# A vision tower on one core: attention that forms its scores a second time by keys, two fused mixer fronts and a scan with wider jobs

## The chip, the cores and the metric

The kernel runs on one core of one Trainium2 chip, in one launch. The metric is the device time in microseconds (us) of an execution. The engines are PE (TensorE: matrix products and transposes into PSUM), DVE (VectorE), ACT (ScalarE), POOL (GpSimd) and SP (SyncE, which issues transfers). PE's clock is granted at one of two levels, 1.2 or 2.4 GHz; the profile gives it as a share of full speed, 0.50 or 1.00 (a number between is a mean over a stretch).

## What is computed

32 images become 32 x 50 = 1600 tokens of 192 features, and four layers follow, each a mixer and a feed-forward part (ffn), each added to the stream h. Everything is fp32. The diff touches four mixers:

```python
# layer 0 mixer: a bilinear state-space scan, 16 states per feature
bc = x @ W_bc;  delta = softplus(x @ W_dt @ W_dtp + b_dt)
delta = delta * rsqrt(mean(delta * delta) + 1e-6) * rms_scale
dE = soft_clamp(delta, 0.0001, 10.0)             # centre + half_range * tanh(...)
half = 0.5 * dE * A;  denom = 1.0 - half          # A = -exp(A_log)
A_bar = (1.0 + half) / denom;  B_bar = sqrt(dE) * B_sel / denom
Bx = B_bar * 0.5 * (x + x_prev);  h_t = A_bar * h_(t-1) + Bx;  y = sum(C * h) + D * x
# layer 1 (inside its ffn) and layer 2 (its mixer): attention of 12 heads of 16
attn = softmax(q @ k.T * scale)                   # within one image of 50 tokens
out = (attn @ v) @ proj_w + proj_b                # in layer 2 q and k are of unit length first
# layer 3 mixer: 384 inner features
x_s, z = split(rms(x) @ w_in);  xc = silu(conv4(x_s) + conv_b)
B, C, log_dt = split(xc @ w_xproj);  dt = softplus(log_dt @ w_dt + b_dt)
h_t = exp(dt * A) * h_(t-1) + dt * B * xc;  y = (sum(C * h) + D * xc) * silu(z) @ w_out
```

The other parts (patch embedding, layer 1's one-head mixer, the expert layers) are as in the reference, and the diff leaves them.

## The kernel before, in words

`tower` calls the stages one after another. A stage is one or more blocks (`t.block()`): in a block each engine has its own program, they meet only in semaphores (`wait_ge`, `then_inc`), and a block ends for all engines together. So nothing of one block overlaps the next, and the order on an engine is the order in which its program is written; `Fori` is a loop on the engine itself. Tokens are worked in 16 tiles of 100 (two images) or in 4 chunks of 400. `h` and `x` hold tokens on partitions, `xT` holds features on partitions, 96 and 96.

- **Layer 0's front** (`layer0_mixer`, from L695). Block one (L708): per chunk PE forms `bc` (L718), the rank-48 product (L721) and, when ACT has copied that (L741), the rate (L727). Block two (`softplus`, L372, 8 spans of 200 tokens): ln(1+e^z) from Abs, Exp, Ln and one more Exp on ACT (L385 to L398) and five steps on DVE (L405 to L421). Block three (L760): per chunk a square (L766), the mean over features on PE (L781), Sqrt (L768), reciprocal on DVE (L797), two scalings (L800); then over all tokens at once Tanh (L770), clamp (L804), Sqrt (L773) and the input u (L807).
- **The scan** (`scan`, L428). First B and C are split into three bf16 parts (L453 to L459). Then a job is one state of one group of features over a chunk. In layer 0 there are 2 groups of 96 partitions, so 32 jobs a chunk; DVE does three instructions a job: `weigh` (L613), the recurrence (L622) and `read` (L628), with ACT making the decay (L533, L540, L548), POOL one product (L586), and PE spreading B and C over partitions (L493) and summing the states with an identity (L489). In layer 3 there are 3 groups of 128 and 48 jobs.
- **Attention** (`heads_attention`, L1092; layer 1 with unit=False, layer 2 with unit=True). One tile an iteration, two in flight. PE projects q, k, v (L1153, L1154), transposes q and k to 6 blocks (L1160), forms 12 score blocks, four at a time on 16 rows each (L1169); DVE scales, masks and copies the scores to SBUF (L1313) and takes the maximum (L1318), POOL subtracts it (L1130), ACT takes the exponent (L1252), DVE sums (L1331); PE transposes the 12 probability blocks (L1198), ACT copies them (L1268), PE forms probabilities x values with 16 moving columns (L1209); the result is divided by the sums (L1339), transposed (L1216), projected (L1220, L1221) and added (L1347). In layer 2 ACT squares (L1232), DVE sums (L1288) and bounds (L1292) the lengths, and ACT takes their inverse root.
- **Layer 3's front** (`layer3_mixer`, L2005). Per chunk PE forms the 6 input products (L2030), ACT copies three (L2052) and takes silu of three (L2056), DVE does the convolution (L2075, L2077), then silu (L2059), `xproj` (L2035), a copy (L2062), the rate (L2041, L2085), and only then the next chunk. `softplus` follows as a block of its own, then one DVE product over all tokens (L2097).

## Time and profile before

| what | us |
|---|---|
| median of three runs (3040.43 to 3058.68) | 3053.26 |
| the profiled execution | 3052.19 |
| its span in the trace | 3050.1 |
| PE busy, share of the span | 2350.0, 77% |
| DVE busy | 1462.9, 48% |
| ACT busy | 980.4, 32% |
| POOL busy | 798.6, 26% |
| granted clock of PE, mean | 0.768 |

A row of a timeline has the start, the time from the first start to the last end of the merged instructions, engine, line, operation, output and inputs, their number, and in brackets the idle time before them and who ended it. PEld is the loading of the stationary operand, which runs beside PE. An fp32 product is two records in the trace. Transposes in fp32 are one record.

### The profile page before, as it was taken

The page shows a single profiled execution, that of the slowest core. Times are in us where ns is not written, and L with a number is a line of the kernel's source. Part 1 is how long each engine was busy: PE and PEld are TensorE (multiplying, and loading weights), DVE is VectorE, ACT ScalarE, POOL GpSimd, SP SyncE. Part 2 cuts the span into 40 slices and gives each one's busy share as a digit, 9 for nine tenths or more (in the row PEclk, how much of TensorE's full clock was granted, in tenths as well). Part 3 has the DMA queues.
Part 4 walks back from the last instruction along what each step waited for, and adds up shares of the span by engine and source line. Part 5 has one row for each costly group of instructions (what it writes and reads, how often), then busy time and mean ns, then how long its engine had stood idle before and what let it go on. Part 6 is the DMA issues. An engine that isn't in the chain of part 4 may idle for free. (4 is left out here: it accounts for less than half of the span.)

```text
span 3050.1 us, 44650 instructions
## 1 busy us (share of the span) xinstructions
PE 2350.0 (77%) x12100; PEld 1653.3 (54%) x12100; DVE 1462.9 (48%) x3230; ACT 980.4 (32%) x2061; POOL 798.6 (26%) x781
## 2 busy tenths in 40 slices
PE   9617997975897597699779954477756993699998
PEld 9302333653675486477536722122245982699987
DVE  4269996234455311555521254899953224422222
ACT  1147784122233233233221223455522221222211
POOL 0004551001122054111100000477602441244443
PEclk9655555876676599555589976799967995799999
DMA  7000000000000386000012100000006761577775
GB/s 205 3 0 1 0 0 0 0 0 0 1 0 0 92 212 152 12 0 0 0 31 62 31 0 0 1 0 0 0 9 193 223 178 42 179 223 223 224 214 128
DMA packets 77597, 201.30 MB, mean 66 GB/s; under 512 B 17685, under 2 KB 47256, under 8 KB 69176
## 3 DMA queue, kind: packets, MB, share of 16 engines
q1 hardware_dynamic: 52472, 169.30, 17.3%
q0 software_dynamic: 25056, 31.22, 6.1%
q8 instruction: 26, 0.43, 0.1%
q14 instruction: 43, 0.35, 0.0%
HBM read 178.81 MB, written 22.91 MB: 66 GB/s over the span
## 5 line engine op out<-in xcount | busy, mean ns | idle before, releaser
L489 PE MATMUL bank<-g,consts 128*128 128x400 f32 (+1 forms) x640 | 388.6, 703 | 64.3 <-DVE g L628 58.6
L1502 POOL DMA_INDIRECT sums<-yblock,put x129 | 206.0, 1597 | 421.0 <-DVE yblock L1765 249.3
L622 DVE TENSOR_TENSOR_SCAN s<-bank,w 128x400 f32<-128x400 f32 (+1 forms) x320 | 313.2, 979 | 3.9 <-POOL w L597 3.8
L1550 PE MATMUL bank<-xTblock,wt 128*128 128x256 f32 (+1 forms) x1464 | 268.4, 341 | 1.7 <-ACT xTblock L1621 1.2
L1755 DVE TENSOR_TENSOR hid<-sa,bank 128x512 f32<-128x512 f32 (+1 forms) x183 | 105.9, 578 | 340.7 <-ACT sa L1642 337.8
L1575 PE MATMUL bank<-wt,hid 128*128 128x192 f32 x1548 | 265.6, 326 | 0.0
L489 PEld LDWEIGHTS bank<-g,consts 128*128 128x128 f32 (+1 forms) x640 | 117.5, 220 | 269.8 <-DVE g L628 260.1
L597 POOL TENSOR_TENSOR w<-u,spreadB 128x400 f32<-128x400 f32 x192 | 192.8, 1036 | 242.1 <-ACT spreadB L568 242.1
L1550 PEld LDWEIGHTS bank<-xTblock,wt 128*128 128x128 f32 x1464 | 237.3, 194 | 23.7 <-issue 1.6
L1575 PEld LDWEIGHTS bank<-wt,hid 128*128 128x128 f32 x1548 | 249.8, 190 | 0.2
L1642 ACT ACTIVATE sa<-bank 128x512 f32<-128x512 f32 (+1 forms) x183 | 93.3, 510 | 482.2 <-PE bank L1561 477.3
L363 PE MATMUL bank<-consts,xs 100*96 100x100 f32 x320 | 71.2, 383 | 168.8 <-DVE xs L316 130.1
L586 POOL TENSOR_TENSOR w<-u,r 96x400 f32<-96x400 f32 x128 | 132.2, 1034 | 258.0 <-ACT r L540 245.6
L1497 POOL DMA_INDIRECT xblock<-table,take x135 | 134.9, 999 | 223.8 <-DVE put L1731 175.2
L493 PE MATMUL bank<-thirds,select 96*96 (+1 forms) x256 | 90.3, 441 | 111.9 <-ACTq L524 66.4
L628 DVE TENSOR_TENSOR g<-s,bank 128x400 f32<-128x400 f32 (+1 forms) x320 | 175.5, 549 | 0.1
L1130 POOL TENSOR_TENSOR scores<-scores,red 100x1200 f32<-100x1200 f32 x34 | 74.6, 2194 | 344.5 <-DVE red L1318 344.5
L552 ACT ACTIVATE bank<-rate,coef 128x392 f32 x192 | 113.2, 591 | 117.8 <-DVE s L622 117.8
L363 PEld LDWEIGHTS bank<-consts,xs 100*96 100x96 f32 x320 | 38.8, 175 | 201.7 <-DVE xs L316 154.8
L1765 DVE TENSOR_SCALAR yblock<-bank,gate 128x192 f32<-128x192 f32 x129 | 49.4, 414 | 205.1 <-PE bank L1575 205.1
L1561 PE MATMUL bank<-xTblock,wt 64*128 64x256 f32 (+1 forms) x1464 | 143.2, 342 | 0.0
L493 PEld LDWEIGHTS bank<-thirds,select 96*96 96x96 bf16 (+1 forms) x256 | 33.0, 129 | 201.0 <-issue 192.0
(364 smaller groups left out, 4062.9 us busy)
## 6 DMA issues: line engine op xcount, KB each, us to landing
wt<-L3f_packed SPq DMA_DIRECT2D x41, 1152.0 KB, 5.8
wt<-L3f_packed SPq DMA_DIRECT2D x41, 576.0 KB, 6.0
wt<-L3m_packed SPq DMA_DIRECT2D x20, 1152.0 KB, 5.6
wt<-L_packed SPq DMA_DIRECT2D x20, 579.0 KB, 4.4
wt<-L3m_packed SPq DMA_DIRECT2D x20, 577.0 KB, 5.9
wt<-L_packed SPq DMA_DIRECT2D x20, 576.0 KB
pixels<-pixels SPq DMA_DIRECT2D x16, 375.0 KB, 4.3
wu<-L_up SPq DMA_DIRECT2D x8, 576.0 KB, 4.6
```

Source lines behind the costliest of these rows:

```text
L489: nc.tensor.matmul(acc[g][0:parts, 0:CHUNK], ident[0:parts, 0:parts], g_[:, j % SLOTS, :], start=(n == 0), stop=(n == STATES - 1)).then_in ...
L493: return nc.tensor.matmul(bank[0:parts, 0:CHUNK], select[:, row:row + 1].to_broadcast([6 * STATES, parts]), thirds[:, at], start=True, sto ...
L552: nc.scalar.activation(rest, rate[:, g, at].rearrange("p (b t) -> p b t", t=SEQ)[:, :, 1:SEQ], ACT.Exp, scale=coef[:, g, n:n + 1]).then_in ...
L586: nc.gpsimd.tensor_tensor(w1[:, j % SLOTS, :], u[:, j % groups, at], r[:, j % SLOTS, :], ALU.mult).then_inc(w1_done, 1)
L597: nc.gpsimd.tensor_tensor(w2[:, j % SLOTS, :], u[:, g, at], spreadB[:, n % 2, :], ALU.mult).then_inc(bu_done, 1)
L622: nc.vector.tensor_tensor_scan(s[:, j % SLOTS, :], decays[j % DECAYS], w2[:, j % SLOTS, :], 0.0, ALU.mult, ALU.add).then_inc(s_done, 1)
L628: nc.vector.tensor_tensor(g_[:, j % SLOTS, :], s[:, j % SLOTS, :], bankC[(j // groups) % 2][0:parts, 0:CHUNK], ALU.mult).then_inc(g_done, 1)
L1497: nc.gpsimd.indirect_dma_start(x[:, b % 2, q - column_of_block[b], :], None, table, bass.IndirectOffsetOnAxis(take[:, q:q + 1], 0)).then_i ...
L1502: nc.gpsimd.indirect_dma_start(t.sums, bass.IndirectOffsetOnAxis(put[:, q:q + 1], 0), y[:, b % 2, q - column_of_block[b], :], None, comput ...
L1550: nc.tensor.matmul(bank[:, n * j:n * (j + 1)], wt[:, v, cols(base, 2 * p + j)], xT[:, v, 0, 0:n], start=(j == 0), stop=False, skip_group_c ...
L1561: last = nc.tensor.matmul(bank[:, n * j:n * (j + 1)], wt[half, v, cols(REST_AT, 2 * p + j)], xT[half, v, 1, 0:n], start=False, stop=True, ...
L1575: last = nc.tensor.matmul(bankY[s], hid[:, m, 128 * s:128 * (s + 1)], wt[:, v, DOWN_AT + DIM * m:DOWN_AT + DIM * (m + 1)], start=(m == 0 a ...
```

## The change

What it does, part by part:

1. **Layer 0's normalise is wide.** `xT` becomes 128 partitions x 2: features 0 to 127, and features 128 to 191 written twice (64 and 64 partitions). Each tile gets one more DVE instruction (64 columns). The row of ones that was set once in `embed` is set by POOL in layer 0's `add_back`.
2. **Layer 0's front is one block** of 7 unrolled steps over 4 chunks: chunk n is projected, n-2 is in softplus, n-3 is scaled. The root of the mean is Exp(-0.5 Ln(mean + 1e-6)) on ACT, reading PSUM; the reciprocal on DVE is gone. Every operation is now on 128 partitions and 800 columns a chunk. x + x_prev is on POOL. Tanh, clamp, Sqrt and u go by chunks.
3. **Layer 0's scan** (`bilinear_scan`) has 24 jobs a chunk: 16 of the first 128 features, and 8 that hold two states of the last 64. B and C are spread once a job, the second kind with a stationary operand `select_pair` made once (96 x 2048), and its states are summed with a folded identity.
4. **Attention** (both layers) forms the scores twice. The first time (L1363, 18 rows: two more carry the mask) only DVE's maximum reads them, from PSUM, and writes it as a column of the wide q. That is transposed again (3 blocks), and the second score product (L1371, 19 rows) has keys as output partitions, with mask and shift in the product, so ACT takes the exponent from PSUM in one instruction of 1200 columns and its result is already transposed. The sums and the outputs are 24 products with a stationary operand of 32 columns (ones, or the padded values) and 100 moving columns at column positions 0, 32, 64, 96 (L1380). The reciprocal is Exp(-Ln) on ACT, the division leaves `aT` ready for three projection products and one for the bias (L1418, L1419). POOL's subtraction, the 12 transposes of probabilities and their copies, the DVE masking, sum and reciprocal, and the transposes of the result are gone. The projection weights arrive by a transfer in this block.
5. **Layer 3's front is one block** of 6 unrolled steps: chunk n projected, n-1 mixed, n-2 in softplus; ACT changes its table twice a step; u is formed by POOL chunk by chunk. Layer 3's scan is unchanged.

```diff
-        self.xT = sb("xT", [HALF + 1, 2, TOKENS + 2 * TILE])
+        self.xT = sb("xT", [128, 2, TOKENS + 2 * TILE])
...
+                        if wide:
+                            nc.vector.tensor_scalar(xs[:, u:u + 1, DIM:LINE], src[:, at, 128:DIM], mv[:, at, 0:1], sd[:, 2, at],
+                                                    ALU.subtract, ALU.mult)
...
+def job_states(j):
+
+    p, r = divmod(j, 3)
+    return (1, (2 * p, 2 * p + 1)) if r == 2 else (0, (2 * p + r,))
...
+                            lhs = select_pair[:, (base + states[0]) // 2].rearrange("p a b -> p (a b)")
+                        return nc.tensor.matmul(bank[:, 0:CHUNK], lhs, thirds[:, at], start=True, stop=True)
...
-                    with act.Fori(0, CHUNKS) as c:
-                        at = bass.ds(CHUNK * c, CHUNK)
-                        act.sem_inc(t.passed, 1)
-                        nc.scalar.activation(sq[:, :, at], rate[:, :, at], ACT.Square).then_inc(squared, 1)
-                        act.wait_ge(eps_done, c + 1)
-                        nc.scalar.activation(rms[:, 1, :], rms[:, 0, :], ACT.Sqrt).then_inc(root, 1)
...
+                        c = n - 2
+                        if live(c):
+                            act.wait_ge(soft, c + 1)
+                            nc.scalar.activation(sq[:, c], rate[:, :, at(c)], ACT.Square).then_inc(squared, 1)
+                        c = n - 3
+                        if live(c):
+                            act.wait_ge(meant, c + 1)
+                            nc.scalar.activation(rms[:, 0, c % 2, :], bank_mean[c % 2][:, 0:CHUNK], ACT.Ln, bias=w["eps6"]).then_inc(logged, 1)
...
+                def score_turned():
+                    for g in range(GROUPS):
+                        for j in range(4):
+                            rows = slice(32 * j, 32 * j + DEEP)
+                            last = nc.tensor.matmul(bankS[j][0:TILE, TILE * g:TILE * (g + 1)], qkT[rows, 1, g, :], shiftedT[rows, g, :],
+                                                    start=True, stop=True)
+                    last.then_inc(scoredT, 1)
+
+                def weigh(v):
+                    for bank in (bankR, bankO):
+                        for g in range(GROUPS):
+                            for j in range(4):
+                                rows = slice(32 * j, 32 * (j + 1))
+                                last = nc.tensor.matmul(bank[rows, TILE * g:TILE * (g + 1)],
+                                                        ones[:, 0:2 * HEAD] if bank is bankR else v_[:, v, 4 * g + j, :], pT[:, j, g, :],
+                                                        start=True, stop=True, tile_position=(0, 32 * j))
+                    last.then_inc(weighed, 1)
...
+                        act.wait_ge(scoredT, n + 1)
+                        nc.scalar.activation(pT[:].rearrange("p j g n -> p j (g n)"), wholeS, ACT.Exp).then_inc(exp_done, 1)
+                        act.wait_ge(weighed, n + 1)
+                        nc.scalar.activation(logs[:].rearrange("p g n -> p (g n)"), bankR[:, 0:GROUPS * TILE], ACT.Ln).then_inc(sums_logged, 1)
+                        act.wait_ge(sums_logged, n + 1)
+                        nc.scalar.activation(inv[:], logs[:], ACT.Exp, scale=-1.0).then_inc(inv_done, 1)
+                        square(n + 2)
+                        take_shifted(n + 1)
+                        root(n + 2)
...
+                        take_qkT(n + 1)
+                        highest(n + 1, 1 - u)
+                        dve.wait_ge(inv_done, n + 1)
+                        nc.vector.tensor_tensor(aT[:].rearrange("p g n -> p (g n)"), bankO[:, 0:GROUPS * TILE],
+                                                inv[:].rearrange("p g n -> p (g n)"), ALU.mult).then_inc(a_done, 1)
+                        lengths(n + 2)
+                        take_qk(n + 2, u)
+                        take_v(n + 2, u)
+                        dve.wait_ge(out_done, n + 1)
...
-                        pe.wait_ge(rate_done, G * c + G)
...
+                @block.gpsimd
+                def _(pool):
+                    for c in range(CHUNKS):
+                        pool.wait_ge(soft, c + 1)
+                        nc.gpsimd.tensor_tensor(u[:, :, at(c)], rate[:, :, at(c)], xc[:, :, at(c)], ALU.mult)
```

**Where instructions stand, first place: PE, one tile of the attention loop of layer 1.** The numbers are those of the listing; the first listing is the kernel before, with L1169 the scores, L1153 and L1154 the projection, L1198 the transposes of probabilities, L1160 those of q and k, L1209 the values, L1216 to L1221 the output.

```order
305 L1169 MATMUL bank<-qkT 100x100 x12
...
307 L1153 MATMUL bank<-consts,xtile 100x384
308 L1154 MATMUL bank<-consts,xtile 100x384
309 L1153 MATMUL bank<-consts,xtile 100x192
310 L1154 MATMUL bank<-consts,xtile 100x192
...
313 L1198 MATMUL bank<-consts,scores 100x100 x12
314 L1160 MATMUL bank<-consts,wide 128x100 x6
...
316 L1209 MATMUL bank<-v,probsT 100x16 x4
...
321 L1216 MATMUL bank<-consts,a 96x100 x2
322 L1220 MATMUL bank<-consts,aT 100x192
323 L1221 MATMUL bank<-consts,aT 100x192
```

In the changed kernel L1371 is the second score product, L1363 the first, L1380 the 24 narrow products, L1349 the transposes of q, k and shifted q:

```order
318 L1371 MATMUL banks<-shiftedT,qkT 100x100 x12
...
320 L1349 MATMUL banks<-consts,wide 128x100 x6
321 L1363 MATMUL banks<-qkT 100x100 x12
322 L1380 MATMUL banks<-probsT,ones 32x100 x12
323 L1380 MATMUL banks<-probsT,v 32x100 x12
...
325 L1342 MATMUL banks<-consts,xtile 100x384
326 L1343 MATMUL banks<-consts,xtile 100x384
327 L1342 MATMUL banks<-consts,xtile 100x192
328 L1343 MATMUL banks<-consts,xtile 100x192
329 L1349 MATMUL banks<-consts,wide 128x100 x3
330 L1418 MATMUL banks<-wproj,aT 100x192 x3
331 L1419 MATMUL banks<-wproj,ones 100x192
```

The 12 transposes of probabilities are gone, a second set of 12 score products has come, and the transposes of q and k stand ahead of the first scores of the next tile.

**Second place: PE, layer 3's front, the first two chunks.** Before, with L2030 the input products, L2035 `xproj` and L2041 the rate; these rows are a loop's body, run once a chunk:

```order
646 L2030 MATMUL bank<-xT,consts 128x400
...
648 L2030 MATMUL bank<-xT,consts 128x400 x11
...
651 L2035 MATMUL bank<-xc,consts 33x400
...
653 L2035 MATMUL bank<-xc,consts 33x400
...
655 L2035 MATMUL bank<-xc,consts 33x400
...
657 L2041 MATMUL bank<-bc_203,consts 128x400 x3
```

Now, unrolled, with L2222 and L2231 the input products of x and z, L2240 `xproj` and L2248 the rate:

```order
628 L2222 MATMUL banks<-xT,consts 128x400 x6
629 L2231 MATMUL banks<-xT,consts 128x400 x6
630 L2222 MATMUL banks<-xT,consts 128x400 x6
631 L2231 MATMUL banks<-xT,consts 128x400 x6
632 L2240 MATMUL banks<-xc,consts 33x400 x3
633 L2248 MATMUL banks<-bc_211,consts 128x400 x3
```

The 12 input products of the second chunk now stand ahead of the first chunk's `xproj` and rate.

## Rows read from the trace of the kernel before

**Rows 1.** Stretches of stages: us; busy PE, PEld, DVE, ACT, POOL; clock; DMA.

```profile
111.50:228.70 117.20, 46.31 (x64) 12.36 (x64) 51.35 (x71) 37.56 (x56) 0.00 (x0) 0.50 0.00 0
228.70:236.50 7.80, 0.00 (x0) 0.00 (x0) 7.22 (x7) 0.00 (x0) 0.00 (x0) 0.50 0.00 0
242.80:491.50 248.70, 235.25 (x381) 77.02 (x381) 240.94 (x391) 195.91 (x377) 130.45 (x127) 0.50 0.00 0
757.80:965.20 207.40, 186.18 (x1332) 141.88 (x1332) 100.40 (x186) 60.19 (x118) 44.03 (x36) 0.70 0.00 0
1243.50:1480.60 237.10, 215.90 (x1332) 167.92 (x1332) 128.64 (x240) 74.63 (x172) 44.02 (x36) 0.57 0.00 0
1792.80:1930.00 137.20, 61.31 (x144) 29.26 (x144) 67.29 (x102) 43.30 (x69) 0.00 (x0) 0.70 0.00 0
1950.00:1962.00 12.00, 9.55 (x25) 3.27 (x24) 12.00 (x19) 6.39 (x12) 9.02 (x10) 1.00 0.00 1
```

**Rows 2.** Timeline of layer 0's front.

```profile
112.12 2.87 PE L718 MATMUL bank<-xT,consts 96*32 x4 [1.49 <-PEq L712]
...
119.04 2.95 PE L727 MATMUL bank<-low,consts 48*96 x4 [1.22 <-ACT low L741]
...
196.66 2.65 DVE L797 RECIPROCAL rms<-rms 96x400 f32<-96x400 f32 x1 [0.60 <-ACT rms L768]
...
225.06 3.49 DVE L807 SCALAR_TENSOR_TENSOR u<-u,sq 96x3200 f32<-96x3200 f32 x1 [2.94 <-ACT sq L773]
```

**Rows 3.** Groups of instructions of the scans: xcount, then busy us and mean ns.

```profile
L622 DVE TENSOR_TENSOR_SCAN s<-bank,w 128x400 f32<-128x400 f32 (+1 forms) x320 | 313.2, 979 | 3.9 <-POOL w L597 3.8
...
L628 DVE TENSOR_TENSOR g<-s,bank 128x400 f32<-128x400 f32 (+1 forms) x320 | 175.5, 549 | 0.1
```

**Rows 4.** Timeline of layer 0's scan, PE.

```profile
350.94 0.87 PE L493 MATMUL bank<-thirds,select 96*96 x2
...
351.61 3.22 PE L489 MATMUL bank<-g,consts 96*96 96x400 f32 x4
```

**Rows 5.** Timeline of layer 1's attention, PE.

```profile
859.29 0.79 PE L1169 MATMUL bank<-qkT 16*100 16x100 f32 x24
...
860.00 1.60 PE L1153 MATMUL bank<-consts,xtile 97*100 97x384 f32 x2
...
863.96 2.21 PE L1198 MATMUL bank<-consts,scores 100*100 100x100 f32 x12
...
866.92 2.21 PE L1209 MATMUL bank<-v,probsT 100*100 100x16 f32 x24
...
871.98 1.09 PEld L1169 LDWEIGHTS bank<-qkT 16*100 16x100 f32 x24 [0.48 <-issue]
...
871.98 1.34 PE L1169 MATMUL bank<-qkT 16*100 16x100 f32 x24
```

**Rows 6.** Groups of instructions of attention.

```profile
L1313 DVE SCALAR_TENSOR_TENSOR scores<-bank,consts 100x300 f32<-100x300 f32 x136 | 52.8, 450 | 6.3 <-PE bank L1169 6.3
...
L1318 DVE TENSOR_REDUCE red<-scores 100x12 f32<-100x1200 f32 x34 | 47.7, 1403 | 1.2
...
L1252 ACT ACTIVATE scores<-scores 100x1200 f32<-100x1200 f32 x34 | 40.7, 1197 | 0.0
...
L1245 ACT ACTIVATE qkT<-bank 128x300 f32<-128x300 f32 x72 | 26.3, 418 | 65.3 <-PE bank L1160 65.1
...
L1292 DVE TENSOR_SCALAR norm<-norm 100x24 f32<-100x24 f32 x18 | 14.9, 829 | 0.6
```

**Rows 7.** Timeline of layer 3's front, all engines.

```profile
1793.51 1.28 ACT L2047 ACT_TABLE_LOAD   x1 [0.27 <-PEq L99]
...
1794.03 10.62 PE L2030 MATMUL bank<-xT,consts 96*128 x24 [2.15 <-PEq L2024]
...
1806.58 2.17 PE L2035 MATMUL bank<-xc,consts 128*33 x6 [1.93 <-ACT xc L2059]
...
1924.60 5.16 DVE L2097 TENSOR_TENSOR u<-rate,xc 128x4800 f32<-128x4800 f32 x1 [0.32 <-PEq L99]
```

More of the change, by code:

```diff
@@ L271, in _, with normalise @@
                     last.then_inc(multiplied, 1)
-def normalise(t, src, eps, *, keep=None, centred=True, gain=None, bias=None, feature_major=True):
+def normalise(t, src, eps, *, keep=None, centred=True, gain=None, bias=None, feature_major=True, wide=False):
     nc = t.nc
@@ L390, in _ @@
[L390 to L398 removed]
+                act.wait_ge(a_zero, 1)
@@ new lines, in _ @@
+            @block.gpsimd
+            def _(pool):
+                pool.sem_inc(w1_done, SLOTS)
+                with pool.Fori(0, CHUNKS) as c:
+                    at = bass.ds(CHUNK * c, CHUNK)
+                    for j in range(jobs):
+                        pool.wait_ge(r_done, c * jobs + j + 1 + SLOTS)
+                        pool.wait_ge(w2_done, c * jobs + j + 1)
+                        pool.sem_inc(t.passed, 1)
+                        nc.gpsimd.tensor_tensor(w1[:, j % SLOTS, :], u[:, group(j), at], r[:, j % SLOTS, :],
+                                                ALU.mult).then_inc(w1_done, 1)
@@ L769, in _ @@
-                    act.wait_ge(scaled, 2 * CHUNKS)
-                    nc.scalar.activation(sq[:], rate[:], ACT.Tanh, scale=1.0 / REACH,
-                                         bias=w["clamp"][0:HALF, :]).then_inc(tanh_done, 1)
-                    act.wait_ge(clamped, 1)
-                    nc.scalar.activation(sq[:], rate[:], ACT.Sqrt).then_inc(rooted, 1)
-                @block.tensor
-                def _(pe):
-                    with pe.Fori(0, CHUNKS) as c:
-                        at = bass.ds(CHUNK * c, CHUNK)
-                        pe.wait_ge(squared, c + 1)
-                        for k in range(2):
-                            last = nc.tensor.matmul(t.bank[0][0:HALF, 0:CHUNK], w["mean"][:], sq[:, k, at],
-                                                    start=(k == 0), stop=(k == 1))
-                        last.then_inc(meant, 1)
+                    nc.scalar.preload_act_table_set("natural_log_exp_and_others")
@@ new lines, in _ @@
+                    nc.scalar.preload_act_table(ACT.Tanh)
+                    for c in range(CHUNKS):
+                        act.wait_ge(scaled, 2 * c + 2)
+                        nc.scalar.activation(sq[:, c], rate[:, :, at(c)], ACT.Tanh, scale=1.0 / REACH, bias=w["clamp"]).then_inc(tanh_done, 1)
+                    nc.scalar.preload_act_table(ACT.Sqrt)
+                    for c in range(CHUNKS):
+                        act.wait_ge(clamped, c + 1)
+                        nc.scalar.activation(sq[:, c], rate[:, :, at(c)], ACT.Sqrt).then_inc(root_done, 1)
@@ L1156, in project, with turn_ @@
                     last.then_inc(projected, 1)
[L1158 to L1165 removed]
+                def turn_(v, first, out, at, done):
+                    for g in range(GROUPS):
+                        last = nc.tensor.transpose(out[:, at + TILE * g:at + TILE * (g + 1)],
+                                                   wide[:, v, first + 4 * g:first + 4 * g + 4, :].rearrange("p h e -> p (h e)"),
+                                                   ident[0:TILE, 0:TILE])
+                    if done is not None:
+                        last.then_inc(done, 1)
@@ L2064, in _ @@
+                @block.gpsimd
+                def _(pool):
+                    for c in range(CHUNKS):
+                        pool.wait_ge(soft, c + 1)
+                        nc.gpsimd.tensor_tensor(u[:, :, at(c)], rate[:, :, at(c)], xc[:, :, at(c)], ALU.mult)
                 @block.vector
```

896 lines of the change are left out of this document (538 added, 358 removed).

## The prediction

> **What bounds the kernel now.** The page says only that PE is busy for 77% of the span at a mean clock of 0.768. The change touches stages, so I read the busy time and the clock of each stage first [rows 1], then their timelines, then the groups of instructions for single durations. In the order of the program:
>
> - Layer 0's front, 111.5 to 228.7, takes 117.2 us and no engine is busy for half of it [rows 1]. It is a chain: products, then softplus, then the mean, each behind a block's end. PE's products run at the low level (4 records of 400 columns in 2.87 us, 0.67 each), one after another with a copy between [rows 2]; a reciprocal on DVE costs 2.65 and its successors wait for it, and the last four steps run whole over all tokens, as u does in 3.49 [rows 2].
> - Layer 0's scan, 242.8 to 491.5, is DVE's: 240.9 busy of 248.7 [rows 1]. It has 4 x 32 = 128 jobs, 1.94 us each, of which the recurrence is 0.98 and the read 0.55 [rows 3], the rest a like multiplication. ACT has 195.9 / 128 = 1.53 a job, POOL 1.02 [rows 1]. PE is at clock 0.50 throughout.
> - The two attentions, 207.4 and 237.1 us, are PE's: 186.2 and 215.9 busy, at clocks 0.70 and 0.57; DVE has 100 and 129, ACT 60 and 75 [rows 1]. The reader is to see in rows 5 that PE's work doubles in time when the clock falls: the same 24 score records last 0.79 and 1.34.
> - Layer 3's front, 1792.8 to 1930.0, takes 137.2 with PE busy 61 and DVE 67 [rows 1]: again a chain, ended by 5.16 on DVE alone [rows 7].
>
> These stages sum to 955 us with the 7.8 of the splitting [rows 1]. Expert stages, normalisations, layer 1's own mixer and layer 3's scan stay, and I leave them at their time.
>
> **The change part by part.** All terms are against the profiled execution, 3052.2, which is 1.1 below the median of 3053.3.
>
> *Layer 0's scan.* Partitions cost DVE nothing (the recurrence's two forms, 96 and 128 partitions, are in one group with mean 979 [rows 3]), so 24 jobs replace 32. Per chunk 62.2 us now (248.7 / 4), about 59 for jobs at 1.84 and 3.2 between chunks. After: 4 x (24 x 1.84 + 3.2) = 189.4, so **-59**. ACT's 1.53 and POOL's 1.02 stay below. PE is nearer: two spreads a job at 0.33 (0.87 for two with the latency) and one sum of 1.33 (4 records in 3.22 hold two sums, 2.67, and what lies between) [rows 4] make 2.0 at the low clock, above DVE's 1.84. Layer 3's scan shows what follows there: on 128 partitions, once PE had no gaps, the clock is 1.00 and DVE is busy 12.00 of 12.00 (the last of [rows 1]). I take the same here. If the clock stayed low, 4 x (24 x 2.0 + 3.2) = 205, a loss of 15. Making `select_pair` (2048 columns on DVE) costs about 2.2, by the rate of the 3200 columns in 3.49 [rows 2]; the extra instruction of the wide normalise about 0.16 x 16 = 2.5. Together **+4.7**. The row of ones on POOL lies beside `add_back` and is hidden.
>
> *Layer 0's front.* I follow the new program at the low clock. Per chunk PE has 12 records, 8.0 us, and waits 1.4 for ACT's two copies: three steps end at 28.4. The fourth step starts with the mean of chunk 0, which waits behind Abs, Exp and Exp on ACT, five steps on DVE and the square: 8.3 (ACT 0.85 and DVE 0.9 to 1.0 for 800 columns, by the rates in rows 2 and 6). Then 2.7 for the mean, 9.4 for the products, 8.3 again: 57.1. Two draining steps of 7.0, 5.4 to the last scaling, and a tail of 9.9 (two table loads of 1.28 [rows 7], Tanh and Sqrt by four chunks): 86. Against 117.2: **-31**. At the high clock the same chain gives 68; without any overlap it stays 117, which are the two ends.
>
> *Attention, layer 1.* PE's list for one tile at the high clock: first and second scores 0.62 each (issue of 24 records; 0.79 with the end), 9 transposes 0.9 (12 in 2.21 at the low clock, so 0.092 each at the high one), projection 1.96 (half of the 3.96 between 860.00 and 863.96, less the overlap), output 4 products of 192 columns 1.28, all from rows 5. The 24 narrow products are 48 records of 100 columns. No row shows products at column positions. From below: the score records, four at a time on different rows, go out every 26 ns, so 48 take 1.3. From above: one after another at 83 ns, 4.0. I take 1.9, near the first, because the scores are the nearest row for four operands side by side. Sum 7.3. PE then waits about 1.2 for DVE's two copies of 300 columns (0.43 to 0.45 [rows 6]), since the next tile's first scores need them. That makes 8.5, and with changes of the array's form 9.0. DVE has two copies, the maximum 1.40, the scaling, three copies and an add, about 4.1; ACT 1.20 for the exponent and three of 0.42 to 0.45 [rows 6], 2.6: neither is the bound. Start to first add, in series and partly at the low clock: 30. So 30 + 15 x 9.0 = 165 against 207.4: **-42**. POOL's 2.2 us subtraction and DVE's mask go, and nothing waited for is put in their place but the copies.
>
> Row-form products cost something at each change: before the scores PEld sits idle for 0.48 in the row of 871.98 [rows 5]. The Trainium skill says on this (TensorEngine Tiling (Array Packing), Key Properties) that changing the tiling mode drains the engine; the trace agrees with 0.48. By it the new tile has five such changes where the old has two; I have 0.5 for the three in the 9.0.
>
> *Attention, layer 2.* The same list, and PE also waits for the lengths: square, sum, bound (0.83 [rows 6]), two activations, scaling, then q, k and v, all after the projection, some 3.2 us of which the output and second scores cover 1.9. Period 10.5, and with part of the tiles at the low clock, because of these gaps, 11.2. Start 34: 34 + 15 x 11.2 = 202 against 237.1: **-35**.
>
> *Layer 3's front.* At the high clock PE has 8.0 + 2.0 + 2.0 a chunk (24 records in 10.62 with the rise of the clock inside, 6 in 2.17 [rows 7]); ACT has two table loads, six copies or silus and three Abs at 0.50, four of 1.19 and one copy, about 12.3. In order these give steps of 8.3, 13.3, 13.3, 13.9, 12.6, 18.4 and 3.1 for the last product on POOL: 83. All at the low clock the steps are PE's and the sum is 126. Between them by the clock, at 0.8: 83 + 43 x 0.25 = 94. Against 137.2, with room for 1 us: **-42**. POOL's product in place of 5.16 on DVE is hidden but for its last quarter.
>
> Sum: -59 + 4.7 - 31 - 42 - 35 - 42 = -204, so 3052.2 - 204 = **2848**.
>
> **The rivals.**
>
> *A. Attention stays at the low clock.* For it: it is at 0.57 in layer 2 now [rows 1]. Against: the list now is full of transposes and 16-column products; the new one has 100 or more moving columns nearly everywhere. PE's list is then 13.8, the period 15.3 and the starts 32 and 37: 261.5 and 267 for 207.4 and 237.1, so +54 and +30 in place of -42 and -35: 3052 - 127 + 84 = 3009. The Trainium skill (TensorE: Matmul & The Clock Gate, Part 4: PE-mode transpose) says that transposes don't count as busy for the clock in the same way; here 12 + 6 of them and low clocks go together, which agrees, and speaks for the change.
>
> *B. The narrow products go one after another, at the high clock.* For it: they use all 100 rows, and no row here shows such a form side by side; the value products before, also on 100 rows, took 92 ns a record for 16 columns [rows 5]. Then 4.0 for 1.9, periods 11.1 and 13.3: 196.5 and 233.5, -11 and -4: 3052 - 127 - 15 = 2910. The Trainium skill (TensorE: Matmul & The Clock Gate, Part 3: Packing small matmuls) says that a weight load overlaps a running product only where the row group differs, which speaks against this change, though it also reports a gain for column packing.
>
> *C. The fronts don't overlap.* Each engine's list is in order, and a late chunk can hold an early one. Then the two blocks keep their 117 and 137: -73 is lost, 2921.
>
> *D. Slower.* One mechanism: the narrow products in a row and at the low clock, 48 x 0.167 = 8.0 us a tile on PE, which then is the bound. Periods 20.2 with starts of 38 and 43: 341 and 346, +242, less 127: 3167. It decides from a period of 16.5 (both attentions at 572 = 444.5 + 127), that is from 4.3 us for the narrow group. Against it: PE with no gaps has got the high clock in layer 3's scan.
>
> **How the numbers follow.** Forecast 0.62 (own range 2800 to 2890), A 0.10, B 0.12, C 0.11, D 0.03, and 0.02 for a loss that I have not seen. A measurement of this kernel tells about 1% from no change. The range reaches from 2795 (both fronts and scan at the high clock: 18 and 11 less, layer 1's tile at 8.3) over B and C and halfway to A, to 2960. Faster by over 1% holds in all but D and part of the last: 0.95, same 0.02, slower 0.03.
>
> **What would show it right or wrong.** The scan's stretch 190 us with DVE busy nearly all of it; the front's 86; the tiles of attention 9 and 11 us apart with the clock above 0.8; the 48 narrow records in under 2.5 us; layer 3's front 94. The forecast is wrong if narrow records start over 80 ns apart, if the clock in attention is under 0.7, or if PE waits for ACT's table loads in layer 3's front for longer than the 12.3 us of ACT's list allows.

## The result, and the profile after

The changed kernel takes 2839.76 us (median of four runs, 2836.61 to 2842.46), the kernel before 3046.85 beside it (four runs): a ratio of 0.9317, 95% interval 0.9279 to 0.9356. Forecast were 2848 and a range of 2795 to 2960. The profiled execution has a span of 2836.3 us, 213.8 less than before, PE busy for 2164.2 (76%) and a mean clock of 0.834 (0.768 before).

The stretches of the changed stages, as in [rows 1]: us; busy PE, PEld, DVE, ACT, POOL; clock; DMA. In order: layer 0's front, the splitting, layer 0's scan from its first recurrence, attention of layer 1 and of layer 2, layer 3's front.

```profile
115.20:201.90 86.70, 49.23 (x64) 11.98 (x64) 32.62 (x45) 35.80 (x53) 5.93 (x4) 0.50 0.00 0
201.90:210.90 9.00, 0.00 (x0) 0.00 (x0) 8.36 (x8) 0.00 (x0) 0.00 (x0) 0.50 0.00 0
217.20:403.80 186.60, 137.22 (x381) 45.45 (x381) 181.95 (x295) 145.89 (x281) 97.47 (x95) 0.95 0.00 0
670.90:837.20 166.30, 145.69 (x1985) 110.65 (x1985) 67.11 (x124) 41.14 (x66) 8.48 (x21) 0.81 0.01 3
1117.70:1309.60 191.90, 159.30 (x1985) 119.77 (x1985) 82.06 (x178) 57.13 (x120) 8.51 (x21) 0.75 0.01 2
1627.50:1713.20 85.70, 55.20 (x144) 25.82 (x144) 61.93 (x81) 50.45 (x67) 14.15 (x4) 0.80 0.00 0
```

Set against the terms of the forecast:

| term | before | forecast | measured | difference forecast / measured |
|---|---|---|---|---|
| layer 0's front | 117.2 | 86 | 86.7 | -31 / -30.5 |
| layer 0's scan | 248.7 | 189.4 | 186.6 | -59 / -62.1 |
| splitting and wide normalise | | | 9.0 for 7.8; 18.5 for 15.2 | +4.7 / +4.5 |
| attention, layer 1 | 207.4 | 165 | 166.3 | -42 / -41.1 |
| attention, layer 2 | 237.1 | 202 | 191.9 | -35 / -45.2 |
| layer 3's front | 137.2 | 94 | 85.7 | -42 / -51.5 |
| all other stages | | | | 0 / +12 |

The last line is the rest of -213.8. The largest part of it is layer 2's ffn, whose code the diff doesn't touch: 279.1 us before, 284.5 now (from its first normalising instruction to that of layer 3).

Layer 0's scan first, a steady piece of it: the recurrence (L546) follows itself after 1.84 us, and PE (spreads L448, sum L465) is done long before.

```profile
387.06 0.98 DVE L546 TENSOR_TENSOR_SCAN s<-banks,w 128x400 f32<-128x400 f32 x1
...
387.29 0.33 PE L448 MATMUL banks<-thirds,select_pair 96*128 x1 [0.15 <-DVE g L552]
...
387.46 0.83 PE L465 MATMUL banks<-g,consts 128*128 128x400 f32 x2
...
388.65 0.33 PE L448 MATMUL banks<-thirds,select 96*128 x1 [0.36 <-DVE w L540]
...
388.90 0.98 DVE L546 TENSOR_TENSOR_SCAN s<-banks,w 128x400 f32<-128x400 f32 x1
```

The sum takes 0.83 here at the high level, not 1.33. At the low level PE's 2.0 a job would, by the forecast's sum, have been the bound; at the clock of 0.95 it isn't, as in layer 3's scan in [rows 1]. The forecast says of that row that PE "had no gaps", but its PE is busy for 9.55 of 12.00 us, and here for 137.2 of 186.6: in both scans PE waits in most jobs, 0.15 to 0.42 us at a time, and the clock stays high nearly all the time.

Now attention. One tile of layer 1 with the clock high, PE and the copy it waits for (L1371 second scores, L1349 transposes, L1363 first scores, L1380 the narrow products, L1342 and L1343 projection, L1418 and L1419 output):

```profile
720.20 0.69 PE L1371 MATMUL banks<-shiftedT,qkT 19*100 19x100 f32 x18
...
720.82 0.73 PE L1349 MATMUL banks<-consts,wide 100*128 100x100 f32 x6
...
721.98 0.46 DVE L1505 COPY qkT<-banks 128x300 f32<-128x300 f32 x1
722.50 0.79 PE L1363 MATMUL banks<-qkT 18*100 18x100 f32 x24 [0.94 <-DVE qkT L1505]
723.21 0.72 PE L1380 MATMUL banks<-probsT,ones 100*32 100x100 f32 x24
...
723.75 0.70 PE L1380 MATMUL banks<-probsT,v 100*32 100x100 f32 x24
724.38 0.89 PE L1342 MATMUL banks<-consts,xtile 97*100 97x384 f32 x2
...
727.98 0.32 PE L1419 MATMUL banks<-wproj,ones 1*100 1x192 f32 x1
728.14 0.69 PE L1371 MATMUL banks<-shiftedT,qkT 19*100 19x100 f32 x18
```

From one group of second scores to the next it is 728.14 - 720.20 = 7.94 us. The 48 narrow records go out from 723.21 to 724.38, 1.17 us, 24 ns each. PE idles once, 0.94, for DVE's copies. The next tile meets the fall of the clock:

```profile
730.43 0.79 PE L1363 MATMUL banks<-qkT 18*100 18x100 f32 x24 [0.94 <-DVE qkT L1505]
...
731.15 1.08 PE L1380 MATMUL banks<-probsT,ones 100*32 100x100 f32 x24
...
731.99 1.25 PE L1380 MATMUL banks<-probsT,v 100*32 100x100 f32 x24
733.16 1.60 PE L1342 MATMUL banks<-consts,xtile 97*100 97x384 f32 x2
...
739.38 0.69 PE L1371 MATMUL banks<-shiftedT,qkT 19*100 19x100 f32 x18
```

The same records now last 1.08 and 1.25, and 1.60 for 0.89; this tile takes 11.24. In layer 1 nine of the 15 distances between additions are 7.94, four 11.2 and two 9.6; a long one follows two short ones, or one. In layer 2 one of 8.77 and one of 11.7 alternate from the sixth addition on (mean 10.50), and PE waits twice a tile, for DVE's v as well:

```profile
1227.40 0.71 PE L1349 MATMUL banks<-consts,wide 100*128 100x100 f32 x6 [0.78 <-DVE v L1500]
1229.05 0.79 PE L1363 MATMUL banks<-qkT 18*100 18x100 f32 x24 [0.94 <-DVE qkT L1505]
1229.76 1.23 PE L1380 MATMUL banks<-probsT,ones 100*32 100x100 f32 x24
```

So the forecast for layer 1 (period 9.0, measured 9.03 on the mean; start 30, measured 30.5) was right by luck: two errors cancel. What makes the clock fall, and what it costs, is the question of the experiments.

### The profile page after: what moved, and what is told of

It is laid out like the page before. It is cut to its first block and busy times, and to the rows that moved or that the text cites. A ratio compares the mean times of both kernels' runs of the same rounds, so it can differ in the third digit from the quotient of the medians.

```text
span 2836.3 us, 45725 instructions
## 1 busy us (share of the span) xinstructions
PE 2164.2 (76%) x13406; PEld 1541.7 (54%) x13406; DVE 1301.1 (46%) x2981; ACT 897.3 (32%) x1857; POOL 717.6 (25%) x728
## 5 line engine op out<-in xcount | busy, mean ns | idle before, releaser
L1734 PE MATMUL banks<-xTblock,wt 128*128 128x256 f32 (+1 forms) x1464 | 268.9, 341 | 1.7 <-ACT xTblock L1805 1.2
L1939 DVE TENSOR_TENSOR hid<-sa,banks 128x512 f32<-128x512 f32 (+1 forms) x183 | 105.2, 579 | 352.6 <-ACT sa L1826 206.8
L1759 PE MATMUL banks<-wt,hid 128*128 128x192 f32 x1548 | 266.8, 327 | 0.0
L1759 PEld LDWEIGHTS banks<-wt,hid 128*128 128x128 f32 x1548 | 249.2, 190 | 2.0 <-DVE hid L1939 0.2
L1734 PEld LDWEIGHTS banks<-xTblock,wt 128*128 128x128 f32 x1464 | 236.3, 194 | 24.6 <-issue 1.8
L632 PE MATMUL banks<-g,consts 128*128 128x400 f32 x384 | 184.8, 572 | 60.8 <-DVE g L771 56.8
L765 DVE TENSOR_TENSOR_SCAN s<-banks,w 128x400 f32<-128x400 f32 x192 | 188.6, 982 | 4.8 <-POOL w L740 4.8
L695 ACT ACTIVATE banks<-rate,coef 128x392 f32 x192 | 113.2, 591 | 118.4 <-DVE s L765 118.4
L1745 PE MATMUL banks<-xTblock,wt 64*128 64x256 f32 (+1 forms) x1464 | 143.3, 342 | 0.0
L1745 PEld LDWEIGHTS banks<-xTblock,wt 64*128 64x128 f32 x1464 | 116.1, 187 | 23.0 <-issue 12.2
```

The costliest lines, as they stand in the source:

```text
L632: nc.tensor.matmul(acc[g][0:parts, 0:CHUNK], ident[0:parts, 0:parts], g_[:, j % SLOTS, :], start=(n == 0), stop=(n == STATES - 1)).then_in ...
L695: nc.scalar.activation(rest, rate[:, g, at].rearrange("p (b t) -> p b t", t=SEQ)[:, :, 1:SEQ], ACT.Exp, scale=coef[:, g, n:n + 1]).then_in ...
L765: nc.vector.tensor_tensor_scan(s[:, j % SLOTS, :], decays[j % DECAYS], w2[:, j % SLOTS, :], 0.0, ALU.mult, ALU.add).then_inc(s_done, 1)
L1734: nc.tensor.matmul(bank[:, n * j:n * (j + 1)], wt[:, v, cols(base, 2 * p + j)], xT[:, v, 0, 0:n], start=(j == 0), stop=False, skip_group_c ...
L1745: last = nc.tensor.matmul(bank[:, n * j:n * (j + 1)], wt[half, v, cols(REST_AT, 2 * p + j)], xT[half, v, 1, 0:n], start=False, stop=True, ...
L1759: last = nc.tensor.matmul(bankY[s], hid[:, m, 128 * s:128 * (s + 1)], wt[:, v, DOWN_AT + DIM * m:DOWN_AT + DIM * (m + 1)], start=(m == 0 a ...
```

## The experiments

"Stretch" is the time from an attention's start to its last addition, and "unread products" are products whose result nobody reads. Before's time was taken beside each set, so ratios are against before.

**e1: the old attention in the changed kernel.** heads_attention and its weights are those of before, all else is the changed kernel.

> The changed kernel with the attention of before in both layers (its projection weights among the constants again). If the parts of the change are independent: attention stretches back at 207 and 237 us, against 166.3 and 191.9 of the changed kernel, so 86 us more than 2839.8, 2926. Rival, an interplay: the ffn of layer 2, whose code is the same, took 279.1 us before and 284.6 in the changed kernel; if that comes from the new attention ahead of it, it returns to 279 and the time is 2920.

Measured: 2916.47 us, ratio 0.9567 (0.9543 to 0.9591). Stretches of 202.9 and 235.3. The new attention is thus worth 77 us of the 207, where 86 were expected; the fronts and the scan are most of the rest. The old stretches are 6 us shorter here than 207.4 and 237.1, so the parts are independent to within that and some 3 us outside of the attentions. Layer 2's ffn took 285.2, so the new attention ahead of it is not what made it longer. Over all profiled kernels of this study it has two values, 279.1 to 280.3 (before, e5, e11, e12) and 284.5 to 286.6 (the others), with the same code. The clock changes there for the first 100 us or so. In the four traces with the lower value it is high from 106 or 107 us of the stretch on; in the others only from 110 to 113, and in all of these but e8 it is low once more near 261.

**e2: the narrow products in another order.**

```diff
-                        for g in range(GROUPS):
-                            for j in range(4):
+                        for j in range(4):
+                            for g in range(GROUPS):
```

> Loop order of the 24 narrow products turned round: three in a row at one column position instead of four at four positions. If the distance of 24 ns between records comes from four column positions side by side, the 48 records take 3 to 4 us instead of 1.17, at the high clock: 2 to 2.8 us a tile, 32 tiles, 64 to 90 us more, 2904 to 2930. Rival: any product with a stationary operand of 32 columns goes out at 24 ns; then the records stay at 1.2 us and the time within 1% of 2840.

Measured: 2885.13 us (0.9456, 0.9417 to 0.9496), 45 more than the changed kernel. The tile's 48 records take 2.04 us, 703.21 to 705.25:

```profile
703.21 1.05 PE L1380 MATMUL banks<-probsT,ones 100*32 100x100 f32 x20
...
704.02 0.27 PE L1380 MATMUL banks<-probsT,v 100*32 100x100 f32 x1
704.07 0.28 PE L1380 MATMUL banks<-probsT,ones 100*32 100x100 f32 x2
...
705.25 0.89 PE L1342 MATMUL banks<-consts,xtile 97*100 97x384 f32 x2
```

The order matters, so the position does; but the distance is 42 ns, where 3 to 4 us for the 48 meant 62 to 83, and the time is below the 2904 that I expected at least. The first record with v starts ahead of the last ones with ones, which stand before it in the program: records of one position wait for each other while a later position already starts. The 45 us are not the distance alone. It costs 0.87 a tile (the short tile of layer 1 is 8.81), some 27 us; the rest is the clock, which from the first to the last addition is 0.84 in layer 1 and 0.65 in layer 2, for 0.87 and 0.81 in the changed kernel. Yet in layer 2 PE idles less than there: between 1240 and 1290 only the wait of 0.94 is left, once in 13.5 us. So the length of PE's waits alone doesn't tell what the clock does.

**e3: unread products in the place of idle time.**

```diff
+                def fill(times):
+                    for _ in range(times):
+                        nc.tensor.matmul(bankR[0:TILE, GROUPS * TILE:GROUPS * TILE + DIM], ones[:], wproj[0:TILE, 0, :], start=True, stop=True)
...
                         score_turned()
+                        if unit:
+                            fill(2)
...
                         turn_qk(1 - u)
+                        fill(3)
```

> Products whose result nobody reads (ones x 192 columns, 0.32 us each at the high clock) while PE would idle: three behind the six transposes in both layers, and two more ahead of them in layer 2. Theory: the clock falls every third tile (layer 1) and every second (layer 2) because PE idles there, 0.94 us a tile and 0.94 + 0.78. Then it stays high: tiles of 7.95 and 8.77 us, stretches of 150 and 166 instead of 166.3 and 191.9, 2798. Rival: the fall has another cause (the transposes, the row forms, or too much work at the high clock); then the pattern stays and the time is 2840 to 2855.

Measured: 2791.82 us (0.9139, 0.9106 to 0.9171), 48 less than the changed kernel, with more work on PE; the two stretches give 40 of it. From the second addition on the tiles follow each other after 7.94 us in layer 1, and from the third on after 8.76 in layer 2. The stretches:

```profile
671.80:822.40 150.60, 144.87 (x2081) 114.21 (x2081) 67.11 (x124) 41.12 (x66) 8.46 (x21) 0.90 0.01 3
1097.10:1264.90 167.80, 157.77 (x2145) 123.53 (x2145) 81.93 (x178) 56.20 (x120) 8.46 (x21) 0.91 0.01 3
```

The clock, 0.81 and 0.75 in the changed kernel, is low only in the start: from the first addition on it is 1.00. The unread products lie in time that PE idled before and cost nothing.

**e4: plain products for the nine transposes.**

```diff
-                        last = nc.tensor.transpose(out[...], wide[...], ident[0:TILE, 0:TILE])
+                        last = nc.tensor.matmul(out[...], wide[...], ident[0:TILE, 0:TILE], start=True, stop=True)
```

> The nine transposes of a tile as plain products with the identity, 0.167 us each instead of 0.092 at the high clock, so 0.67 us a tile more. Rival theory: transposes are what PE's clock falls on (before, 18 a tile stood with clocks of 0.57 and 0.70; now 9 a tile stand with 0.75 and 0.81). Then the clock stays high, tiles of 8.6 and 9.4 us, stretches of 159 and 175, 2816. Theory of the idle time: the pattern stays, 0.7 to 1.3 us more a tile in 32 tiles, 2862 to 2880.

Measured: 2904.38 us (0.9507, 0.9475 to 0.9538), 65 more, above both expectations. Layer 1 still has two short tiles (9.17) and one long (12.4), layer 2 one of 9.7 and two of 13.9: the falls stay while the wait of 0.94 stays, and in layer 2 they are more frequent. The short tile grew by 1.23, not 0.67: twelve records take 1.58 where six transposes took 0.73, each with the end.

```profile
761.28 1.58 PE L1349 MATMUL banks<-consts,wide 100*128 100x100 f32 x12
...
763.80 0.79 PE L1363 MATMUL banks<-qkT 18*100 18x100 f32 x24 [0.94 <-DVE qkT L1505]
```

**e5: unread products in layer 0's front too.** In PE's list three products of 200 columns ahead of the wait for low_done, 15 (8 in the last two steps) ahead of that for squared, into a bank of the mean that is free. The attention is that of e3.

> e3 and products whose result nobody reads in layer 0's front as well: three of 200 columns while PE waits for ACT's copies, 15 ahead of each mean of steps 2 and 3, 8 ahead of the two last. The front's 86.7 us stood at clock 0.50 all along. Theory: the chain there holds PE's records at the low level (12 records, 8.0 us a chunk), so at the high level it takes 68 to 74 us, 2776. Rival: ACT's and DVE's steps set the pace and the unread products only delay the means; then 87 or more, 2792 to 2800.

Measured: 2788.63 us (0.9121, 0.9099 to 0.9143), the same as e3 within the measurement; the front took 83.8. PE had nothing idle from 115.45 on, yet the clock stayed low for some 40 us:

```profile
137.81 6.00 PE L882 MATMUL banks<-xT,consts 128*32 128x400 f32 x8
...
149.00 7.87 PE L874 MATMUL banks<-xT,consts 128*128 128x200 f32 x30
...
156.72 1.70 PE L900 MATMUL banks<-sq,consts 128*128 128x400 f32 x4
158.35 3.25 PE L882 MATMUL banks<-xT,consts 128*32 128x400 f32 x8
...
171.57 1.81 PE L900 MATMUL banks<-sq,consts 128*128 128x400 f32 x4 [1.95 <-ACT sq L935]
178.26 1.80 PE L900 MATMUL banks<-sq,consts 128*128 128x400 f32 x4 [1.98 <-ACT sq L935]
```

After the rise, the step from one mean to the next took 14.9 us (156.72 to 171.57) for 20.5 before, so PE's low level was on the chain there; in the last steps the distance is 6.69, as without the unread products, so ACT's and DVE's steps set it. What the high level gave was mostly spent by the products at the low one: the first mean came 4.1 us later than in the changed kernel.

**e6: the disputed cost by itself.** Ahead of the narrow products of e3 stand 12 products at column position 0 (L1418), 12 in turn at four positions (L1421) and 6 with 100 stationary columns (L1424), all with 100 moving columns and unread.

> e3 with 30 more products a tile ahead of the narrow ones, results unread, to measure the disputed cost by itself at the high clock: 12 with 32 stationary columns, all at column position 0; 12 the same in turn at positions 0, 32, 64, 96; 6 with 100 stationary columns. In turn: 24 records at 24 ns as in the kernel, 0.6 us. At one position: 83 ns a record if it is busy for the whole record (2.0 us for 24), 42 ns if e2's mean of 42 us per thousand records is its distance (1.0 us). With 100 columns: 83 ns a record.

One run, 2918.51 us. One tile:

```profile
752.68 2.16 PE L1418 MATMUL banks<-consts,ones 100*32 100x100 f32 x23
754.60 0.29 PE L1421 MATMUL banks<-consts,ones 100*32 100x100 f32 x3
754.68 0.25 PE L1418 MATMUL banks<-consts,ones 100*32 100x100 f32 x1
754.71 0.73 PE L1421 MATMUL banks<-consts,ones 100*32 100x100 f32 x21
755.37 1.30 PE L1424 MATMUL banks<-consts,ones 100*100 100x100 f32 x12
756.61 0.72 PE L1384 MATMUL banks<-probsT,ones 100*32 100x100 f32 x24
```

At one position the records follow each other after (754.60 - 752.68) / 23 = 83 ns; in turn the last 21 take 0.66, 31 ns; with 100 stationary columns 1.24 / 12 = 103 ns, not the 83 that I expected. So the gain of the narrow form is the four positions, and e2's 42 is half of 83, as where two positions overlap. The clock is 1.00 from the first to the last addition of both attentions, so the levels don't blur this.

**e7: the old attention with its idle time filled.** On e1, `fill(2)` of 192 columns ahead of the wait for aT_done, and in layer 1 also ahead of that for a_done.

> e1 (the attention of before) with unread products where its PE idles, 192 columns each: two ahead of the wait for the divided result (layer 1 alone) and two ahead of the wait for its transposed copy (both layers). If idle time alone lowers the clock, the old attention rises to the high level as well: PE's list of a tile is then about 9.5 us, stretches of 170 and 185 instead of 203 and 235, 2830. If its 18 transposes and 24 products of 16 columns hold the clock down by themselves, it stays near 0.73 and 0.57 and the time within 15 us of 2916.

Measured: 2932.7 us (0.9597, 0.9575 to 0.962), 16 more than e1; stretches of 220 and 233 at clocks of 0.70 and 0.62. As a whole it doesn't separate the causes: where the clock does rise, other waits appear, for DVE.

```profile
817.24 1.24 PE L1393 MATMUL banks<-consts,scores 100*100 100x100 f32 x12 [0.91 <-DVE scores L1511]
819.14 0.73 PE L1355 MATMUL banks<-consts,wide 100*128 100x100 f32 x6 [0.66 <-DVE wide L1503]
```

It does show that the old attention at the high level waits for DVE's masking copies (L1511), which the change took away. And between two such waits, which come in four tiles of layer 1, there is a piece in which PE never idles and the clock is low all the same:

```profile
821.00:862.00 41.00, 41.00 (x253) 33.33 (x252) 17.94 (x33) 10.26 (x19) 7.64 (x7) 0.58 0.00 0
```

The old list of products thus has a low clock without any idle time. Which of its products do that is the question of e9 and e10.

**e8: useful work in the gap.** On e3, the output products of the third group and the bias, with the addition, stand one tile later, behind the six transposes; one unread product is left there.

> e3 with useful work in the place of unread products: two of the four output products of a tile, 0.64 us, stand behind the transposes of the next tile, one unread product stays there, and DVE adds the result one step later. If PE's list sets the tile, it shortens by 0.64 us, tiles of 7.3 and 8.1 us, 20 us over both layers, 2772. Rival: the later addition, for which the narrow products wait, takes the place of the gap; then 2790 or more.

Measured: 2799.74 us (0.9172, 0.9147 to 0.9195), not better than e3. Layer 1's tile fell to 7.62, by half of what I expected, since one unread product of 0.32 was now on the path. Layer 2's rose from 8.76 to 9.07. There the rival held, and the two layers cancel (0.32 less and 0.31 more a tile).

**e9 and e10: what else pulls the clock down.** On e3, where PE has no idle time, ahead of the narrow products:

```diff
+                        for _ in range(12):
+                            nc.tensor.transpose(bankR[0:TILE, 300:400], ones[:], ident[0:TILE, 0:TILE])
...
+                        for _ in range(12):
+                            nc.tensor.matmul(bankR[0:TILE, 300:316], ones[:], ident[0:TILE, 0:HEAD], start=True, stop=True)
```

> e3 (no idle time left on PE, clock high all along, tiles of 7.94 and 8.76 us) with 12 transposes more a tile, results unread, as many as the old attention had for its probabilities. If transposes pull the clock down by themselves, it falls below 0.9 and the tiles are 10 us or more. If only idle time does, it stays high and the tiles grow by 12 x 0.092 = 1.1 us, to 9.05 and 9.87, 36 us in all: 2828.

> e3 with 12 products more a tile of 16 moving columns and 100 stationary ones, results unread: half the records of the old value products (24 took 2.21 us there). If such short products pull the clock down, it falls below 0.9 and the tiles are 11 us or more. If only idle time does, it stays high and the tiles grow by 2.2 us, to 10.15 and 11.0, 70 us in all: 2863.

One run each, 2826.03 and 2920.18 us. With 12 more transposes the tiles are 9.10 and 9.93 and a piece of layer 1's stretch has PE busy all the time at 1.00; the clock doesn't fall:

```profile
740.00:780.00 40.00, 40.00 (x616) 32.90 (x609) 17.55 (x32) 11.03 (x17) 1.41 (x4) 1.00 0.00 0
```

With 12 short products layer 1 had 10.16 between additions only from the fifth to the fifteenth; then, in the last tile, the clock fell again during the short products, with PE busy for the 40 us before, and the tile took 15.0. Layer 2 never settled (11.0 to 14.9 a tile), though PE never idled:

```profile
1220.00:1280.00 60.00, 60.00 (x670) 48.42 (x669) 21.45 (x47) 16.13 (x35) 1.76 (x5) 0.80 0.00 0
```

So products of 16 moving columns pull the clock down without any idle time, and transposes of 100 columns don't. The time of e10 is 57 us above the 2863 expected with the clock high. The 12 products are 24 records, as many as the old attention had a tile [rows 5], not half of them as the expectation says; its price of 2.2 us a tile was right (10.16 for 7.94).

**e11 and e12: is it the width?** e5 and e3 with layer 0's projection products on 128 stationary columns instead of 32 and 48.

```diff
-                                    last = nc.tensor.matmul(bank[0:rows, 0:CHUNK], w[name][0:part, k, :], t.xT[0:part, k, at(n)],
+                                    last = nc.tensor.matmul(bank[:, 0:CHUNK], t.consts[0:part, first:first + 128], t.xT[0:part, k, at(n)],
```

> e5 with the projection's products of layer 0's front on 128 stationary columns instead of 32 and 48 (the columns more are neighbouring constants, their rows of the result are not read); records of the same length. In e5 PE had no idle time from 115 to 165 us and its clock rose only at about 154, some 5 us into the first long run of products on 128 x 128. Theory: the clock counts how much of the array a product uses; then it rises within some 5 us of the start, PE's 12 records a chunk take 4 us, the front 66 to 76 us instead of 83.8, 2774 to 2782. Rival: the width doesn't matter; then the front stays at 84 and the time at 2789.

> e3 with the same 128 stationary columns in layer 0's front and no unread products there. If the width matters and PE's waits there are short enough (1.0 us of 11 in the first two steps), the clock rises in the first steps, falls again in the waits of 7 us, and the front takes 78 to 84 us instead of 86.7; if the width doesn't matter, or the waits undo it, 86.7 and 2792.

Measured: 2787.86 (0.9155, 0.91 to 0.9211) and 2792.93 us (0.9158, 0.911 to 0.9206), equal to e5 and e3. The records were not of the same length: eight take 6.56 us instead of 5.98. In e11 the rise lies inside the 30 unread products again (7.51 us from 151.58), in e12 the clock is 0.50 throughout; the fronts take 85.6 and 89.1 us against 83.8 of e5 and 86.7. The number of stationary columns is not it. The theory that the used part of the array counts is not refuted as a whole, though: e11 widened the columns and left the rows. Half of the projection's records use 64 rows and the rate's 48; layer 3's input products use 96, the unread ones here 128. No run changes the rows alone. Why the clock stays low through 40 us of unbroken products in layer 0's front, and rises within the first chunk of layer 3's, stays open.

## Why the prediction was right, and where it was not

**The total** was 8 us too high (2848 for 2839.8), by errors of both signs: 3 too much in the scan, 10 in layer 2's attention and 9 in layer 3's front, against 12 that the untouched stages took more. That it came out so near is in part luck. The lower bound was added up wrongly: the terms named for 2795, 18, 11 and 15 x 0.7, give 2808; nothing hangs on it here.

**Layer 0's front and scan** came out nearly as worked out: the front's steps (57.1 for four, 7.0 for the draining ones, a tail of 9.9) were the list's at the low level. Measured, PE waits 0.97 for the copies (forecast 1.4) and 7.23 for the square (8.3), and means follow after 6.69. The splitting and the wide normalise cost 4.5 for 4.7, but 1.2 and 3.3 for 2.2 and 2.5. Rival C, that a list in order would hold an early chunk up, did not happen in either front.

**Attention, the narrow group.** The step "I take 1.9, near the first" was too careful: 1.17, below even the 1.3 of the lower bound. The reasoning by the nearest row, four operands side by side at 26 ns, was right, and e6 shows why: 83 ns at one position, 31 in turn. Rival B, with its 4.0, is the price of one position for all, 48 x 83 ns; its ground, that the records use the same 100 rows, made no difference.

**Attention, the period.** "8.5, and with changes of the array's form 9.0" is the step that failed: a high tile takes 7.94. Of the 1.06 too much, 0.7 is the narrow group and 0.3 the wait of 1.2 that is 0.94. The 0.5 for the changes of form is about used up: the rest of PE's list takes 7.94 - 0.94 - 1.17 = 5.83 for the 5.4 of the sum, and what is left over beside the records' distances lies in good part at such changes, about 0.1 between L1363 and L1380 and between L1380 and L1342, and about 0.2 where L1371 follows the output products. The Trainium skill (TensorEngine Tiling (Array Packing), Key Properties) has a drain at each such change; in this trace that is 0.1 to 0.2 at the high level, not the 0.48 of [rows 5]. The second error has the other sign: I had the clock high in every tile of layer 1, and it falls in six of 15. The wait at DVE's copies I had priced as waiting, but not as a clock; e3, which fills it, has no falls. In layer 2 the price of a high tile, 10.5, was too high by 1.7, and 0.7 for the low ones too little (measured 1.7 on the mean); 202 was forecast for 191.9.

**Rival A's ground.** Against A I had that the old list is full of transposes and 16-column products. e4 takes the transposes away and the falls stay; e9 adds twelve and none comes. What goes with the falls here is idle time in attention (e3) and products with 16 moving columns (e10); e2 and e4 have more falls than the changed kernel with no more idle time, which neither explains. The new list does run higher, 0.81 and 0.75 for 0.70 and 0.57, but only half of the ground for it holds. By the rule of the Trainium skill that I cited there (TensorE: Matmul & The Clock Gate, Part 4: PE-mode transpose), transposes don't count as busy in the same way. Then e9's 21 a tile, some 1.9 us at 0.09, would weigh like idle time, of which 0.94 a tile went with falls; the measured 1.00 disagrees.

**Layer 3's front.** The step "between them by the clock, at 0.8: 83 + 43 x 0.25" failed. The clock was 0.80 as taken, but most of its low part lies where PE waits or is not the bound; the stretch is 85.7, near the 83 of the chain at the high level. PE is on the path at the low level in two places. The first 12 input records last 6.60 for the 4.19 of the next 12, and near the end the last `xproj` costs 2 us:

```profile
1673.72 2.20 PE L2240 MATMUL banks<-xc,consts 128*33 128x400 f32 x6
...
1685.94 4.21 PE L2240 MATMUL banks<-xc,consts 128*33 128x400 f32 x6 [7.16 <-ACT xc L2265]
```

**The untouched stages** were left at their time, a term put at nothing; they took 12 us more, 5.4 of them in layer 2's ffn. There the longer time goes with a clock that rises some 5 us later, and e1 excludes that the new attention does it. What decides between 280 and 285 was not found.

**The fastest versions** are e3, e5, e11 and e12, 2787.9 to 2792.9 us, one and the same by this measurement and 1.7 to 1.8% under the changed kernel.

## What to carry to other kernels

Ask of every short wait of PE not only how long it is but what the clock does behind it: here, with 0.94 us of waiting in a tile of 8, six tiles of 15 took 1.6 to 3.3 us more, and products that nobody reads, put into the waits, gave 48 us back. Not every wait does that: in layer 0's scan PE waits in most jobs and the clock is 0.95. Narrow products gained here when successive ones stood at different column positions (83 ns a record at one, 24 to 31 in turn at four); write the loop so that the position changes fastest. And weigh a low clock only where PE is on the path: the mean clock of a stretch doesn't show where that is.

## What the runs showed that I had not expected

- With the wait filled, the clock stayed at 1.00 for all tiles behind the start in both attentions (e3), though PE did more.
- Records at different column positions overtake each other (e2, e6), so two positions overlap even with three products in a row at each: 42 ns a record, where one position alone gives 83 and four in turn 24 to 31.
- Twelve products of 16 moving columns a tile held layer 2's clock at 0.80 with PE busy for 60.00 of 60.00 us (e10). In layer 1 the same twelve let it rise after five tiles, until the last; why the layers differ is open.
- In layer 0's front 40 us of products without a gap did not raise the clock, with 32 and 48 or with 128 stationary columns (e5, e11); the rows used were the same.
- A transpose as a plain product costs 0.14 us more at the high level (e4: 1.23 us for nine).
- With three narrow products in a row at each position, layer 2's clock fell to 0.65 with one wait of 0.94 in 13.5 us (e2), for 0.81 with more waiting in the changed kernel; this stays open.
